# FiLM attention block and expert-choice block on one core: the order of the second layer's weight preparation and of the first norm

## The chip, the cores and the metric

The kernel runs on 1 core of one Trainium2 chip, as one launch. The metric is the device time in microseconds (us) of one execution; lower is better. Several executions of a kernel are given by their median.

A core has TensorE (PE, matrix products and transposes, into eight PSUM banks), VectorE (DVE), ScalarE (ACT), GpSimd (POOL) and SyncE (SP, which here only issues DMAs). The engines run side by side and are tied to each other by semaphores that the kernel sets and waits for by hand.

## The reference

x has the shape (2, 512, 128): two batches of 512 tokens of width 128. Two layers follow each other.

Layer 0: RMS norm, FiLM with a scale and a shift that come from `cond`, one attention head of width 128, its projection, the residual; then RMS norm, FiLM, and a GELU MLP 128 to 512 to 128 with its residual.

Layer 1, cut to what matters here:

```python
shift = silu(t) @ W_ada.T + b_ada
h = _ln(x, ln1_g, ln1_b) + shift
qkv = (h @ Wqkv.T).reshape(b, n, 3, H, HD)      # H = 16 heads, HD = 64
q, k = _ln(q, qn_g, qn_b), _ln(k, kn_g, kn_b)   # per head
attn = softmax(q @ k.T / sqrt(HD))              # per head
x = x + (attn @ v) @ Wout.T
```

Then a gate chooses 128 tokens for each of 8 experts (top-k by expert), the experts' two matrices with a GELU run on them, and the weighted results are added back to their tokens. All is float32.

## The kernel before

Every engine has one program, written in the order in which it runs. Tokens are kept in chunks of 128 (four to a batch). The stages are: load, layer 0 norm and FiLM, q, k and v of both batches, an attention loop over eight chunks (`g`), projection, the MLP (`up0`, `down0`), layer 1 norm, a hand-written lead-in to the heads, a loop over 32 units (16 heads by 2 batches), the gate, and the experts. Only what comes up to the lead-in, the first 84 us or so, is touched by the change.

**The start.** ScalarE issues the load of x as one DMA (L562) and squares it in two halves. VectorE sums the squares (`sum_squares`), GpSimd makes rstd (`norm_scale`, L451) behind its constants (L424 to L448), VectorE scales (`scaled`), and TensorE turns the four chunks of a batch (`turn_norm`). ScalarE (batch 0) or VectorE (batch 1) applies FiLM while copying out of PSUM (`into_h`). TensorE turns both batches ahead of the projections (L1292 to L1307), whose results are q0, k0 and v0. SyncE issues every other load in a fixed order (L377 to L394): early rows, film1, q, k, v, broadcast biases, Wqkv, W_ada, eleven pieces of the late rows, and the rest.

**The attention loop of layer 0.** In round g TensorE does `scores0(g)`, `turn0(g - 2)` and `mix0(g - 3)`; in round 1 it also turns the late rows (`late_turns`, L1270), which wait for their DMAs, and in round 3 it makes the products for FiLM 2 and `ada` (`late_products`). VectorE takes the row maximum and scales the probabilities, ScalarE makes the exponentials and copies turned probabilities.

**The weights of layer 1** are prepared in ten banks of 512 columns, n = 0 to 9. Banks 0 to 3 centre the q and k columns of Wqkv with a matrix product (`make_weights`, L1343): 0 and 2 hold heads 0 to 7, 1 and 3 hold heads 8 to 15. Banks 4 and 5 turn Wout (4: the part of heads 0 to 7). Banks 6 to 9 multiply each head's v weights by its part of Wout, with a contraction over 64 rows: 6 and 7 are even and odd heads of the first eight, 8 and 9 of the last eight. ScalarE copies each bank out (`copy_weights`, L594), into `w_hi` for q, k and v banks, and for these VectorE subtracts the copy to give `w_lo` (`weights_low`, L922). In TensorE's order banks 0 to 5 stand in rounds 1 to 6 of the loop, all through PSUM bank 7; bank 6 behind the loop, 7 behind `up0(3)`, 8 and 9 behind `down0(0)` and ahead of `up0(4)`. All ten are ready ahead of the first projection of layer 1.

**The lead-in.** `project(p, ...)` makes q, k and v for a head pair and two chunks, as three products (hi by hi, hi by lo, lo by hi). `piece_square`, `piece_ss`, `piece_scale`, `piece_norm`, `turn_piece`, `piece_affine`, `piece_high` and the low parts turn its result into normalized q and k. `project(0)` and `project(1)` take batch 0, `project(2)` and `project(3)` batch 1. Between the two pairs, batch 1's residual (`block_out(1)`), its centring (GpSimd, L532), its norm and `turn_norm(2, 1)` are done. `keep_busy(n)` does 4n transposes of the identity that nobody reads. `row_max` and `scores` are the first steps of the unit's attention. SyncE loads the experts' weights once the last half of h is split (`h_split` 4), which overwrites the raw weights.

Of the kernel before, what the change touches and what calls it, by code (L numbers as in the profile page):

```python
# [37 lines left out]
def film_attention_then_expert_choice(  # L38
# [35 lines left out]
    with ctx:  # L74
# [163 lines left out]
        proj_in = sem("proj_in")  # L238
# [16 lines left out]
        centring_ready, centre_ready = sem("centring_ready"), sem("centre_ready")  # L255
# [80 lines left out]
        def weight_bank(n):  # L336

            return bank[7] if n < QK_BANKS + WOUT_BANKS else bank[5 + n % 2]
# [10 lines left out]
        def weight_psum(n):  # L349

            return weight_bank(n)[:, :].rearrange("p (h d) -> p h d", d=HD if n < QK_BANKS else D)
# [24 lines left out]
        def _(sp):  # L376
# [27 lines left out]
            sp.wait_ge(wT_copied, W_BANKS + 1)  # L404
# [10 lines left out]
        def _(pool):  # L415
# [24 lines left out]
            pool.wait_ge(centring_ready, 1)  # L440
            link(pool.tensor_scalar(minus_ident[:, :], ident[:, :], -1.0, None, ALU.mult))
# [9 lines left out]
            def norm_scale(k, b, eps):  # L451
                pool.wait_ge(norm_ss, 2 * k + b + 1)
                at = slice(b * NC, b * NC + NC)
                link(pool.tensor_scalar(meansq[:, at], sumsq[:, at], 1.0 / D, eps, ALU.mult, ALU.add))
                pool.tensor_tensor(rstd[:, at], meansq[:, at], minus_half[:, at], ALU.pow).then_inc(norm_rstd, 1)  # L455

            norm_scale(0, 0, EPS0)
            norm_scale(0, 1, EPS0)

            pool.wait_ge(x_loaded, 16)  # L460
            pool.wait_ge(bcast_in, 48)
# [59 lines left out]
            def low_k(p):  # L521
# [39 lines left out]
        def _(act):  # L561
            act.dma_start(x_in[:, :, :], x.rearrange("b (c p) d -> p (b c) d", p=P)).then_inc(x_loaded, 16)  # L562
# [6 lines left out]
            square(x_in, 0)  # L569
            square(x_in, 1)  # L570
# [23 lines left out]
            def copy_weights(n):  # L594
                act.wait_ge(wT_done, n + 1)
                if n < QK_BANKS or n >= QK_BANKS + WOUT_BANKS:
                    act.activation(weight_part(w_hi, n), weight_psum(n), ACT.Copy).then_inc(wT_copied, 1)
                else:
                    m = n - QK_BANKS
                    act.activation(wout_T[:, 4 * m:4 * m + 4, :].rearrange("p c d -> p (c d)"),  # L600
                                   weight_bank(n)[:, :], ACT.Copy).then_inc(wT_copied, 1)
# [16 lines left out]
            copy_weights(QK_BANKS + WOUT_BANKS)  # L618
# [16 lines left out]
            for n in range(HC, 2 * HC):  # L635
                gelu0(n)
            act.wait_ge(wT_done, W_BANKS + 1)
            act.activation(wgate_T[:, :], bank[6][:, 0:E], ACT.Copy).then_inc(wT_copied, 1)
# [94 lines left out]
            for p in range(2):  # L733
                piece_square(p)
                piece_copy(p, p)
                piece_v(p, p)
# [9 lines left out]
            for half in range(2):  # L746
                at = half * (N // 2)
                act.activation(h_T[:, N + at:N + at + N // 2], bank[2][:, at:at + N // 2], ACT.Identity,
                               bias=affine[:, 2, 1, 1:2], scale=affine[:, 2, 0, 1:2]).then_inc(h_act, 1)
            q_high_beside(0, 0)  # L750
# [86 lines left out]
        def _(dve):  # L837
# [25 lines left out]
            sum_squares(0, 1)  # L863
            dve.wait_ge(cols_T, 1)
            dve.tensor_copy(cols[:, 0:EARLY], bank[0][:, 0:EARLY]).then_inc(cols_ready, 1)
            dve.wait_ge(cond_exp, 1)
# [3 lines left out]
            scaled(0, 0, x_in)  # L870

            def film_affine(k, film, fb, w):
                link(dve.tensor_scalar(affine[:, k, 0, :], film[:, 0:B], col(fb), 1.0, ALU.add, ALU.add))
                dve.tensor_scalar(affine[:, k, 0, :], affine[:, k, 0, :], col(w), None, ALU.mult)
                link(dve.tensor_scalar(affine[:, k, 1, :], film[:, B:2 * B], col(fb, 1), None, ALU.add))

            dve.wait_ge(film1_done, 1)
            film_affine(0, bank[4], "film1_b", "norm1_w")
            dve.tensor_copy(silu[:, 0, :], silu[:, 2, :]).then_inc(affine_ready, 1)
# [11 lines left out]
            def late_affine():  # L891
                dve.wait_ge(ada_done, 1)
                film_affine(1, bank[0], "film2_b", "norm2_w")
# [28 lines left out]
            def weights_low(n):  # L922

                dve.wait_ge(wT_copied, n + 1)
                dve.tensor_tensor(weight_part(w_lo, n), weight_psum(n), weight_part(w_hi, n).bitcast(F32),
                                  ALU.subtract).then_inc(w_split, 1)

            for g in range(TC + 1):
# [4 lines left out]
                if 2 <= g <= QK_BANKS + 1:  # L933
                    weights_low(g - 2)
# [18 lines left out]
            weights_low(QK_BANKS + WOUT_BANKS)  # L953
            sum_squares(1, 1)
            scaled(1, 1, x_mid)
            weights_low(QK_BANKS + WOUT_BANKS + 1)
            into_h(1)

# [9 lines left out]
            def split_h(lo, hi):  # L968
# [5 lines left out]
            at = slice(0, NC)  # L974
            block_out(0)
            link(dve.tensor_scalar(centre[:, at], centre[:, at], 1.0 / D, None, ALU.mult))
            dve.tensor_tensor(xn[:, at, :], x_att[:, at, :], spread(centre[:, at], [P, NC, D]), ALU.add)\
               .then_inc(norm_in, 1)
            weights_low(QK_BANKS + WOUT_BANKS + 2)
            sum_squares(2, 0)  # L980
            weights_low(QK_BANKS + WOUT_BANKS + 3)
            scaled(2, 0, xn)
            for half in range(2):
# [92 lines left out]
            scaled(2, 1, xn)  # L1076
            row_max(0, 0)
            dve.wait_ge(h_act, 5)
            split_h(N, N + N // 2)
            row_max(0, 1)  # L1080
            dve.wait_ge(h_act, 6)
            split_h(N + N // 2, TOK)
            row_max(0, 2)
# [157 lines left out]
        def _(pe):  # L1241
# [51 lines left out]
            turn_norm(0, 1)  # L1293
# [3 lines left out]
            for b in range(B):  # L1297
# [4 lines left out]
                pe.matmul(bank[5 + b][:, :], wk0[:, :], hb, start=True, stop=True).then_inc(qkv0_done, 1)  # L1302
                for c in range(NC):
# [39 lines left out]
            def make_weights(n):  # L1343
                dst = weight_bank(n)
                if n == 0:
# [3 lines left out]
                elif n <= QK_BANKS + WOUT_BANKS:  # L1349
                    pe.wait_ge(wT_copied, n)  # L1350
                    pe.wait_ge(w_split, min(n, QK_BANKS))
# [4 lines left out]
                elif n < QK_BANKS + WOUT_BANKS:  # L1356
                    if n == QK_BANKS:
# [428 lines left out]
```

## Time and profile before

| | us |
|---|---|
| median of 3 runs | 422.96 (422.95 to 424.42) |
| the profiled execution | 422.88 |
| its span, first to last instruction | 421.1 |
| TensorE busy | 399.4 (95%) |
| VectorE / ScalarE / GpSimd busy | 275.9 / 284.7 / 193.7 |

The profiled execution is one run of the program with the hardware profiler on. Its span is counted from the first to the last instruction of the core, and all times within the profile are from the span's start. In the profile PE is a matrix product or transpose, PEld a weight load, SPq and ACTq a DMA issued by that engine's queue. A float32 product appears as two instructions (two "passes"), so "x8" is a group of four products. A row of the timeline ends with the idle time ahead of it and what ended that, in brackets.

### The profile page before, as it was taken

What the parts mean: (1) busy time and instruction counts of PE and PEld (TensorE: products, weight loads), DVE (VectorE), ACT (ScalarE), POOL (GpSimd) and SP (SyncE); (2) the same over time, 40 slices, a digit from 0 to 9 for tenths busy, and PEclk for the clock granted to TensorE, in tenths of its full rate; (3) what the DMA queues carried; (4) which work ended last, traced back from release to release, by engine and by line L of the source; (5) the groups of instructions that cost most, each with busy time, mean ns of one, the idle gap of its engine ahead of it and who ended that gap; (6) DMA issues with size and microseconds to landing.
All of it is one profiled execution on the core that took longest, in us unless ns stands there. A gap on an engine that the chain in (4) does not pass through costs nothing.

```text
span 421.1 us, 8341 instructions
## 1 busy us (share of the span) xinstructions
PE 399.4 (95%) x2738; PEld 341.5 (81%) x2738; DVE 275.9 (66%) x648; ACT 284.7 (68%) x532; POOL 193.7 (46%) x203
## 2 busy tenths in 40 slices
PE   6999997899999999999999999999999997789996
PEld 5578666778899889989988998899898786566894
DVE  3666556776666676677676666766775736987733
ACT  3357566677788777778777887777777337759441
POOL 7500416485657756775776577567757000300000
PEclk9999999999999999999999999999999999999999
DMA  5760000191000000000000000000000000000001
GB/s 133 212 133 1 2 2 0 38 362 52 0 3 2 0 2 1 2 2 0 2 2 0 0 0 1 0 0 0 1 0 2 0 2 1 2 2 0 2 2 50
DMA packets 7792, 10.67 MB, mean 25 GB/s; under 512 B 403, under 2 KB 4302, under 8 KB 7758
## 3 DMA queue, kind: packets, MB, share of 16 engines
q1 hardware_dynamic: 6718, 9.73, 8.0%
q10 hardware_dynamic: 1040, 0.52, 0.4%
q8 instruction: 17, 0.28, 0.3%
q14 instruction: 17, 0.14, 0.1%
HBM read 8.68 MB, written 0.52 MB: 22 GB/s over the span
## 4 chain that ended last, share of the span: by engine, by line
PE 81%; DVE 10%; POOL 4%; issue 3%; ACT 2%; DVEq 0%; POOLq 0%; ACTq 0%
PE pair L1489 27%; PE pair L1440 10%; PE pair L1460 7%; PE bank L1479 6%; PE bank L1474 6%; PE pair L1245 4%; PE pair L1715 2%; PE pair L1727 2%; PE pair L1329 1%; PE pair L1405 1%; PE pair L1617 1%; PE bank L1245 1%; POOL rstd L455 1%; PE pair L1672 1%; PE pair L1354 1%
## 5 line engine op out<-in xcount | busy, mean ns | idle before, releaser
L1489 PE MATMUL pair<-v_s,probs_T 128*128 128x129 f32 x1024 | 128.4, 275 | 0.6 <-ACT probs_T L702 0.6
L1489 PEld LDWEIGHTS pair<-v_s,probs_T 128*128 128x128 f32 x1024 | 124.5, 191 | 4.6 <-ACT probs_T L702 0.9
L1016 DVE TENSOR_REDUCE negmax<-pair 128x1 f32<-128x512 f32 x128 | 88.5, 691 | 55.1 <-PE pair L1460 54.8
L702 ACT ACTIVATE probs_T<-bank 128x512 f32<-128x512 f32 x128 | 73.1, 597 | 48.7 <-PE bank L1479 39.4
L500 POOL TENSOR_TENSOR q_s<-kq,k_s 64x512 fp32r<-64x512 f32 x29 | 37.2, 1282 | 73.5 <-DVE k_s L1004 73.5
L1460 PE MATMUL pair<-k_s,q_s 128*128 128x512 f32 x128 | 56.4, 441 | 0.7 <-DVE negmax L1016 0.7
L490 POOL TENSOR_TENSOR qk_rstd<-qk_ms,minus_half 128x8 f32<-128x8 f32 x32 | 53.2, 1661 | 2.6 <-POOL qk_ms L486 0.2
L1474 PE MATMUL bank<-q_s,k_s 128*128 128x512 f32 x128 | 51.1, 399 | 0.0
L1479 PE MATMUL bank<-q_shift,k_low 128*128 128x512 f32 x128 | 50.7, 396 | 0.2 <-DVE q_shift L1023 0.2
L1038 DVE SCALAR_TENSOR_TENSOR x_att<-pair,o_rec,x_att 128x128 f32<-128x128 f32 x128 | 38.6, 344 | 1.1
L500 POOL TENSOR_TENSOR k_low<-kq,k_s 64x512 fp32r<-64x512 f32 x29 | 36.7, 1265 | 2.2
L1023 DVE TENSOR_TENSOR q_shift<-pair,own_chunk 4x512 fp32r<-4x512 f32 x32 | 21.8, 682 | 23.9 <-PE pair L1468 23.9
L509 POOL TENSOR_TENSOR qk_n<-qk_raw,qk_rstd 128x512 f32<-128x512 f32 x28 | 29.3, 1045 | 2.4 <-POOL qk_rstd L490 0.5
L1460 PEld LDWEIGHTS pair<-k_s,q_s 128*128 128x128 f32 x128 | 24.2, 189 | 6.0 <-DVE negmax L1016 3.1
L1479 PEld LDWEIGHTS bank<-q_shift,k_low 128*128 128x128 f32 x128 | 24.0, 188 | 5.7 <-issue 0.4
L650 ACT ACTIVATE qk_sq<-pair 128x512 f32<-128x512 f32 x32 | 19.2, 599 | 12.3 <-PE pair L1440 12.2
L1474 PEld LDWEIGHTS bank<-q_s,k_s 128*128 128x128 f32 x128 | 24.3, 190 | 3.0 <-ACT probs_T L702 0.5
L673 ACT ACTIVATE kq<-pair,cols 128x512 f32<-128x512 f32 x29 | 22.6, 778 | 4.5 <-PE pair L1245 1.4
L1440 PE MATMUL pair<-w_hi,h_hi 128*128 (+1 forms) x64 | 25.5, 398 | 0.0
L1440 PE MATMUL pair<-w_hi,h_lo 128*128 (+1 forms) x64 | 25.2, 394 | 0.0
L1440 PE MATMUL pair<-w_lo,h_hi 128*128 (+1 forms) x64 | 25.1, 391 | 0.0
L990 DVE TENSOR_REDUCE qk_ss<-qk_sq 128x8 f32<-128x512 f32 x32 | 21.7, 677 | 2.7 <-ACT qk_sq L650 2.7
(292 smaller groups left out, 697.5 us busy)
## 6 DMA issues: line engine op xcount, KB each, us to landing
fc_raw<-in_L_cond_fc2s_dram SPq DMA_DIRECT2D x1, 2048.0 KB, 13.8
x_in<-in_x_dram ACTq DMA_DIRECT2D x1, 512.0 KB, 3.9
w<-in_L_cond_mlp_w_dram SPq DMA_DIRECT2D x2, 256.0 KB, 2.9
wout<-in_L_cond_Wout_dram SPq DMA_DIRECT2D x1, 512.0 KB
k_low<-k_low SPq DMA_DIRECT2D x1, 512.0 KB, 8.0
q_shift<-q_shift SPq DMA_DIRECT2D x1, 512.0 KB, 9.4
b_all<-in_L_cond_b2s_dram SPq DMA_DIRECT2D x1, 512.0 KB, 10.9
out_dram<-final SPq DMA_DIRECT2D x2, 256.0 KB, 2.2
```

Source lines behind the costliest of these rows:

```text
L490: pool.tensor_tensor(qk_rstd[:, p_in % 2, :, :].rearrange("p c t -> p (c t)"), qk_ms[:, :, :].rearrange("p c t -> p (c t)"), minus_half[:, ...
L500: pool.tensor_tensor(piece_at(dst, p_in, lo, hi), kq32[lo:hi, :, :], piece_at(k_s, p_in, lo, hi).bitcast(F32), ALU.subtract)\
L509: pool.tensor_tensor(qk_n[:, p_in % 2, :, :, :], qk_raw[:, p_in % 2, :, :].rearrange("p c (t d) -> p c t d", d=HD), spread(qk_rstd[:, p_in ...
L673: act.activation(kq_from(p).rearrange("p h n -> p (h n)"), turn_bank(p)[:, :], ACT.Identity, bias=col("kq_b"), scale=col("kq_g")).then_inc ...
L702: act.activation(probs_T[:, k % 2, :], bank[2 + k % 2][:, :], ACT.Exp).then_inc(exp_done, 1)
L1016: dve.tensor_reduce(negmax[:, c:c + 1], bank[0][:, :], AX, ALU.max, negate=True).then_inc(max_done, 1)
L1038: last = dve.scalar_tensor_tensor(out=at, in0=pair4[:, half, t * (D + 1):t * (D + 1) + D], scalar=o_rec[:, c:c + 1], in1=at, op0=ALU.mult, ...
L1440: last = pe.matmul(banks_of(p)[:, c, :], h_part[:, at:at + P], w_part[:, bass.ds(head, 2), :].rearrange("p h w -> p (h w)"), start=(n == 0 ...
L1460: pe.matmul(bank[0][:, :], q_s[:, pair_at, h, c * P:c * P + P], k_s[:, pair_at, h, :], start=True, stop=True).then_inc(s_done, 1)
L1474: pe.matmul(bank[2 + k % 2][:, :], k_s[:, pair_at, h, at], q_s[:, pair_at, h, :], start=True, stop=False)
L1479: pe.matmul(bank[2 + k % 2][:, :], k_low[:, pair_at, h, at], q_shift[:, pair_at, h, :], start=False, stop=True).then_inc(st_done, 1)
L1489: last = pe.matmul(pair4[:, c // 2, c % 2 * (D + 1):(c % 2 + 1) * (D + 1)], probs_T[:, k % 2, c * P:c * P + P], v_s[:, r % (2 * PAIRS), k, :],
```

## The change

The ten banks are made in another order, `MADE`, and `make_weights`, `copy_weights` and `weights_low` count by the place in this order. Places 0 to 2 (banks 0, 2, 4) stand in rounds 1, 3 and 5 of the attention loop. Places 3 and 4 (V banks 6 and 7) are made together behind `up0(3)` by `make_v_weights(0)`, which goes through head pairs and alternates between the even head (rows 0 to 63) and the odd head (rows 64 to 127), each into a bank of its own. Place 5 (bank 1) stands behind `up0(7)`. Places 6 and 7 (banks 3 and 5) stand behind `project(1)`, and `make_v_weights(1)` (banks 8 and 9) between `turn_piece(0, 0)` and `turn_piece(1, 1)`. `project(3)` waits for all splits. The turn of Wgate gets semaphores of its own.

x comes in two DMAs, one for each batch. GpSimd takes the first two `norm_scale` ahead of five of its constants. VectorE copies the early columns ahead of batch 1's sum of squares and does FiLM ahead of silu. TensorE turns batch 1 between batch 0's k and v projections.

Of `down0(1)` one chunk is done ahead of `turn_norm(2, 0)` and three behind it, all ahead of `project(0)`; before, two stood ahead of `project(0)` and two behind `project(1)`. Batch 1's centring goes from GpSimd to VectorE and, with its sum of squares, ahead of piece 1's. ScalarE squares batch 1 ahead of the second piece. Groups of `keep_busy` are 3, 3, 4 and 1 where they were 3, 9 and 1, 2.

```diff
+        MADE = (0, 2, 4, 6, 7, 1, 3, 5, 8, 9)
+        def weight_bank(i):
+            return bank[(7, 7, 7, 5, 6, 7, 5, 2, 4, 5)[i]]
...
+            norm_scale(0, 0, EPS0)
+            norm_scale(0, 1, EPS0)
             link(pool.tensor_scalar(minus_ident[:, :], ident[:, :], -1.0, None, ALU.mult))
...
             piece_scale(1, 1, 0)
-            at = slice(NC, TC)
-            pool.wait_ge(centre_ready, 1)
-            pool.tensor_tensor(xn[:, at, :], x_att[:, at, :], spread(centre[:, at], [P, NC, D]), ALU.add)\
-                .then_inc(norm_in, 1)
+            norm_scale(2, 1, EPS1)
             low_k(0)
-            norm_scale(2, 1, EPS1)
...
-            act.dma_start(x_in[:, :, :], x.rearrange("b (c p) d -> p (b c) d", p=P)).then_inc(x_loaded, 16)
+            act.dma_start(x_in[:, 0:NC, :], x[0].rearrange("(c p) d -> p c d", p=P)).then_inc(x_loaded, 16)
+            act.dma_start(x_in[:, NC:TC, :], x[1].rearrange("(c p) d -> p c d", p=P)).then_inc(x_second, 16)
...
-                if 1 <= g <= QK_BANKS + WOUT_BANKS:
-                    copy_weights(g - 1)
+                if g in (1, 3, 5):
+                    copy_weights(g // 2)
...
             for n in range(HC):
                 gelu0(n)
-            for n in range(QK_BANKS + WOUT_BANKS + 1, W_BANKS):
-                copy_weights(n)
+            copy_weights(3)
+            copy_weights(4)
+            gelu0(HC)
+            gelu0(HC + 1)
             act.wait_ge(norm_in, 1)
             square(xn, 0)
...
-            piece_affine(0)
+            piece_square(0)
+            piece_copy(0, 0)
             act.wait_ge(norm_in, 2)
             square(xn, 1)
+            piece_square(1)
+            piece_copy(1, 1)
+            copy_weights(6)
+            piece_v(0, 0)
+            piece_affine(0)
+            copy_weights(7)
             q_high(0, 0)
+            piece_v(1, 1)
             piece_affine(1)
...
+            centred(1)
             piece_ss(0)
+            sum_squares(2, 1)
             piece_ss(1)
             piece_norm(0, 0)
-            block_out(1)
-            dve.tensor_scalar(centre[:, NC:TC], centre[:, NC:TC], 1.0 / D, None, ALU.mult).then_inc(centre_ready, 1)
+            weights_low(6)
+            piece_high(0, 0)
             piece_norm(1, 1)
-            piece_high(0, 0)
             low_here(0, HD, q_s).then_inc(q_low_done, 1)
-            sum_squares(2, 1)
+            scaled(2, 1, xn)
...
+            weights_low(8)
+            weights_low(9)
             row_max(0, 2)
...
+            def make_v_weights(eight):
+                first = (3, 8)[eight]
...
+                for k in range(4):
+                    pair_of = 4 * eight + k
+                    for odd in range(2):
+                        part = slice(odd * HD, odd * HD + HD)
+                        last = pe.matmul(weight_bank(first + odd)[:, k * D:k * D + D],
+                                         wqkv_raw[part, 2 * KC + pair_of, :], wout_T[part, pair_of, :],
+                                         start=True, stop=True)
...
-            make_weights(QK_BANKS + WOUT_BANKS + 1)
+            make_v_weights(0)
             turn_norm(1, 1)
             down0(0, range(NC))
-            for n in range(QK_BANKS + WOUT_BANKS + 2, W_BANKS):
-                make_weights(n)
...
+            make_weights(5)
...
+            down0(1, range(1))
             turn_norm(2, 0)
-            down0(1, range(NC // 2))
+            down0(1, range(1, NC))
...
             project(1, 1, 0)
-            down0(1, range(NC // 2, NC))
+            make_weights(6)
+            make_weights(7)
+            pe.wait_ge(norm_in, 2)
+            keep_busy(3, bank[4])
             turn_piece(0, 0)
-            keep_busy(3)
+            make_v_weights(1)
             turn_piece(1, 1)
-            keep_busy(9)
+            pe.wait_ge(v_placed, 2)
+            keep_busy(3, bank[1])
+            turn_norm(2, 1)
+            keep_busy(4, bank[1])
             scores(0, 0, 0)
-            turn_norm(2, 1)
...
-            pe.wait_ge(h_split, 4)
+            pe.wait_ge(w_split, SPLITS)
             project(3, 3, 0)
```

## Rows read from the trace of the kernel before

**Rows 1.** Busy time of the engines, and the granted clock in 40 slices, in tenths.
```profile
PE 399.4 (95%) x2738; PEld 341.5 (81%) x2738; DVE 275.9 (66%) x648; ACT 284.7 (68%) x532; POOL 193.7 (46%) x203
PEclk9999999999999999999999999999999999999999
```

**Rows 2.** Chain of waits, 0 to 90 us: start, duration (us), engine, tile, line.
```profile
17.35 0.86 PE bank L1314 x2
18.21 0.19 PE pair L1275
...
18.65 0.89 PE pair L1354 x8
...
40.62 1.85 PE pair L1329 x16
42.46 1.08 PE pair L1370 x8
...
50.84 3.59 PE pair L1405 x32
...
60.99 1.90 PE pair L1405 x16
62.89 1.40 PE pair L1440 x6
...
81.66 1.39 PE pair L1440 x6
83.05 0.24 PE pair L1460
```

**Rows 3.** Timeline of the start: start, duration, engine, line, operation, tiles.
```profile
4.74 1.15 ACT L566 ACTIVATE sq<-x_in 128x512 f32<-128x512 f32 x2 [2.18 <-DMA x_in<-in_x_dram]
...
6.33 0.23 POOL L448 TENSOR_SCALAR slot_number<-slot_number 128x1 f32<-128x1 f32 x1
...
6.72 5.83 SPq L386 DMA_DIRECT2D wada<-in_L_cond_W_ada_dram  x1
...
18.13 0.14 PEld L1275 LDWEIGHTS pair<-ident,late_rows 46*128 46x128 f32 x1 [0.76 <-DMA late_rows<-in_L_cond_qn_b_dram]
```

**Rows 4.** Timeline of the attention loop and behind it, 20 to 44 us.
```profile
21.05 0.68 DVE L925 TENSOR_TENSOR w_lo<-pair,w_hi 128x512 fp32r<-128x512 f32 x1
...
21.84 0.49 DVE L939 TENSOR_SCALAR p<-p,soft 128x512 f32<-128x512 f32 x1
...
21.88 1.13 PE L1354 MATMUL pair<-centring,wqkv_raw 128*128 128x128 f32 x8 [1.03 <-DVE w_lo L925]
...
42.66 0.69 DVE L854 TENSOR_TENSOR xn<-x_mid,rstd 128x512 f32<-128x512 f32 x1 [1.50 <-POOL rstd L455]
```

**Rows 5.** Timeline of TensorE: the last two V banks, and `slot_weights`.
```profile
54.34 1.71 PE L1370 MATMUL pair<-wout_T,wqkv_raw 64*128 64x128 f32 x16
...
388.31 0.63 PE L1686 MATMUL pair<-onehot,gate_parts 128*32 128x512 bf16 x8
```

**Rows 6.** Line 1686 alone: duration of one in ns, least, median and most.
```profile
L1686 PE MATMUL pair<-onehot,gate_parts x16: 386/392/400, 388.3 to 391.3; 128*32 128x512 bf16 x16
```

**Rows 7.** Timeline of the lead-in, 66 to 78 us, VectorE and GpSimd.
```profile
66.06 1.64 POOL L490 TENSOR_TENSOR qk_rstd<-qk_ms,minus_half 128x8 f32<-128x8 f32 x1
...
70.17 1.04 POOL L532 TENSOR_TENSOR xn<-x_att,centre 128x512 f32<-128x512 f32 x1
70.24 1.52 DVE L996 TENSOR_TENSOR qk_n<-qk_raw,qk_rstd 128x512 f32<-128x512 f32 x1 [0.29 <-POOL qk_rstd L490]
...
75.88 1.76 DVE L854 TENSOR_TENSOR xn<-xn,rstd 128x512 f32<-128x512 f32 x1 [0.91 <-POOL rstd L455]
```

**Rows 8.** Timeline of TensorE: transposes of the identity by `keep_busy`, early and late.
```profile
1.60 3.68 PE L1245 MATMUL pair<-ident 128*128 128x128 f32 x16 [1.60 <-POOL minus_half L427]
...
72.30 4.09 PE L1245 MATMUL pair<-ident 128*128 128x128 f32 x36
```

**Rows 9.** One stretch: busy us of PE, PEld, DVE, ACT, POOL; granted clock; DMA.
```profile
68.00:72.00 4.00, 2.16 (x18) 1.93 (x19) 3.64 (x6) 1.41 (x2) 3.13 (x3) 1.00 0.00 0
```

More of the change, by code:

```diff
@@ L334, in film_attention_then_expert_choice, with splits_ahead @@
         SPLITS = QK_BANKS + V_BANKS
-        def weight_bank(n):
-            return bank[7] if n < QK_BANKS + WOUT_BANKS else bank[5 + n % 2]
+        MADE = (0, 2, 4, 6, 7, 1, 3, 5, 8, 9)
+        assert len(MADE) == W_BANKS
+        def weight_bank(i):
+            return bank[(7, 7, 7, 5, 6, 7, 5, 2, 4, 5)[i]]
+        def splits_ahead(i):
+            return sum(n < QK_BANKS or n >= QK_BANKS + WOUT_BANKS for n in MADE[:i])
         def weight_part(t, n):
@@ L630, in _ @@
                 gelu0(n)
-            for n in range(QK_BANKS + WOUT_BANKS + 1, W_BANKS):
-                copy_weights(n)
+            copy_weights(3)
+            copy_weights(4)
+            gelu0(HC)
+            gelu0(HC + 1)
             act.wait_ge(norm_in, 1)
             square(xn, 0)
[L635 to L638, printed above, removed]
+            gelu0(HC + 2)
+            gelu0(HC + 3)
+            copy_weights(5)
+            act.wait_ge(wgate_done, 1)
+            act.activation(wgate_T[:, :], bank[6][:, 0:E], ACT.Copy).then_inc(wgate_copied, 1)
             act.wait_ge(norm_T, 5)
@@ L862, in _, with film_affine @@
             sum_squares(0, 0)
[L863 removed]
             dve.wait_ge(cols_T, 1)
             dve.tensor_copy(cols[:, 0:EARLY], bank[0][:, 0:EARLY]).then_inc(cols_ready, 1)
+            sum_squares(0, 1)
+            scaled(0, 0, x_in)
+            def film_affine(k, film, fb, w):
+                link(dve.tensor_scalar(affine[:, k, 0, :], film[:, 0:B], col(fb), 1.0, ALU.add, ALU.add))
+                dve.tensor_scalar(affine[:, k, 0, :], affine[:, k, 0, :], col(w), None, ALU.mult)
+                return dve.tensor_scalar(affine[:, k, 1, :], film[:, B:2 * B], col(fb, 1), None, ALU.add)
+            dve.wait_ge(film1_done, 1)
+            film_affine(0, bank[4], "film1_b", "norm1_w").then_inc(affine_ready, 1)
+            dve.wait_ge(affine_ready, 1)
             dve.wait_ge(cond_exp, 1)
@@ L869, in _ @@
             dve.tensor_tensor(silu[:, 2, :], silu[:, 1, :], cols[:, 0:B], ALU.mult).then_inc(silu_ready, 1)
[L870 to L879, printed above, removed]
+            dve.wait_ge(silu_ready, 1)
             scaled(0, 1, x_in)
@@ L972, in split_h, with centred @@
                    .then_inc(h_split, 1)
[L974 to L979, printed above, removed]
+            def centred(b):
+                block_out(b)
+                at = slice(b * NC, b * NC + NC)
+                link(dve.tensor_scalar(centre[:, at], centre[:, at], 1.0 / D, None, ALU.mult))
+                dve.tensor_tensor(xn[:, at, :], x_att[:, at, :], spread(centre[:, at], [P, NC, D]), ALU.add)\
+                   .then_inc(norm_in, 1)
+            centred(0)
             sum_squares(2, 0)
-            weights_low(QK_BANKS + WOUT_BANKS + 3)
             scaled(2, 0, xn)
+            weights_low(5)
             for half in range(2):
@@ L1360, in make_weights @@
                     last = turn4(dst, [wout[:, (at + c) * P:(at + c + 1) * P] for c in range(4)])
-                else:
-                    m = n - QK_BANKS - WOUT_BANKS
-                    if m < 2:
-                        pe.wait_ge(o0_copied, m + 1)
-                    else:
-                        pe.wait_ge(w_split, QK_BANKS + m - 1)
-                    for k in range(4):
-                        h = m // 2 * 8 + 2 * k + m % 2
-                        part = slice(h % 2 * HD, h % 2 * HD + HD)
-                        last = pe.matmul(dst[:, k * D:k * D + D], wqkv_raw[part, 2 * KC + h // 2, :],
-                                         wout_T[part, h // 2, :], start=True, stop=True)
-                last.then_inc(wT_done, 1)
+                last.then_inc(wT_done, 1)
+            def make_v_weights(eight):
+                first = (3, 8)[eight]
+                if eight == 0:
+                    pe.wait_ge(wT_copied, 3)
+                    pe.wait_ge(o0_copied, 2)
+                else:
+                    pe.wait_ge(wT_copied, 8)
+                    pe.wait_ge(w_split, splits_ahead(7))
+                for k in range(4):
[5 more added lines that the diff above has]
+                                         start=True, stop=True)
+                        if k == 3:
+                            last.then_inc(wT_done, 1)
             for g in range(TC + 3):
```

106 lines of the change are left out of this document (54 added, 52 removed).

## The prediction

> **What bounds the kernel now.** I read the page first: TensorE is busy nearly the whole span, at full granted clock [rows 1]. So the question is not which engine is busiest but what TensorE stands behind in the stretch that the change rewrites, from the start to about 84 us. From there on both kernels run the same loop, and what is won by then is carried to the end unchanged. The second view is the chain of waits over that stretch [rows 2]: nearly all of it is TensorE, with short handoffs to the other engines. Its pieces give the landmarks that I compare: the late rows' transposes at 18.21, the last mixes of the first attention ending at 42.46, `down0(0)` ending at 54.43, `project(0)` starting at 62.89, the score of chunk 3 of unit 0 at 83.05, right behind `project(3)`. The third view is the timeline, for who waits inside those pieces [rows 3 to 8].
>
> **Part 1, the start (x in two, Pool's constants later, batch 0 ahead): worth 0.** By itself it works. GpSimd can't take up the first norm before its constants end at 6.56, and ScalarE waits for the whole x [rows 3]. With half of x about 1 us earlier and the norm ahead of the constants, batch 0's projection starts near 8.9; with batch 1's turn behind q and k, all projections end near 14.8 instead of 16.5 (two scores of 0.86 ahead of 18.21 [rows 2]). But after these two scores TensorE comes to the late rows' transposes, which today are released at 18.13 by a DMA, the last of eleven small loads [rows 3]. SyncE issues those behind the load of `wada`, whose issue is held up for 5.83 us behind Wqkv [rows 3]. No issue of SyncE is moved and x carries the same bytes, so the release stays, and the 1.7 us become idle time in front of it. The cover is 1.7 us thick: if no part of the start worked, nothing would be lost. GpSimd's moved constants (from 3.7 to 6.56 today) end near 11, where it starts on x plus bias anyway.
>
> **Part 2, the loop of the first attention: -3.05.** Three of six banks leave it: two of eight passes (0.89 each [rows 2]) and one of four transposes (4 x 0.11 [rows 8]), 2.22 us of TensorE. With them goes the wait of the second bank for the low part of the first, 1.03 us [rows 4]: today both use bank 7 in successive rounds, afterwards a round lies between. VectorE loses two lows of 0.68 [rows 4] and ScalarE three copies, so neither becomes late instead. What is late next is `turn0(1)`: it needs the probability row whose scaling ends at 22.33 behind the first low [rows 4], as today, and restarts TensorE, 0.2 us. Sum 2.22 + 1.03 - 0.2 = 3.05. Played through round by round, `scores0` of round 3 starts at 20.8, of 4 at 25.4, of 5 at 27.6, of 6 at 30.2 (the late affine holds VectorE from 28.2 to 29.4, which makes round 6 wait for a probability row as well), of 7 at 32.5, and the last mix ends at 39.3, 3.1 ahead. The V bank at 42.46 (1.08) leaves too, but it covers a wait: the normalized x_mid arrives at 43.35 [rows 4]. Worth 0.05.
>
> **Part 3, the first V weights, sixteen passes instead of eight behind `up0(3)`: 0.15 gained or 0.7 lost.** Eight passes take 1.08 in the chain [rows 2]; sixteen, one half of the rows after the other, take 1.71 today [rows 5] and 1.8 with the restart. After the change each product alternates between rows 0 to 63 and rows 64 to 127, into different banks. If they overlap, sixteen passes take about 0.9. The nearest row for an overlap is `slot_weights`: eight 512-column matmuls in four column groups take 0.63 together [rows 5] though one alone lasts 0.39 [rows 6], while full-array ones of that length follow each other by 0.23 (six in 1.39 [rows 2]), 1.8 for eight. Column groups do overlap here; row groups never alternate in this trace. Bounds 0.9 and 1.8; I take 0.95, by that row. The Trainium skill says in TensorE: Matmul & The Clock Gate, Part 3, that a weight load passes a running matmul only where the row group differs, and gives a measured 3.07x for four row groups; in TensorEngine Tiling (Array Packing), Tiling Modes, it says that changing the tiling mode drains TensorE. The first would make the block 0.9; the second speaks against short blocks, and today's eight passes, 1.08 against 0.89 for eight full ones, would bear out 0.2 at most.
>
> **Part 4, from `down0(0)` to `project(0)`: 1.15 lost.** The two V banks in front of `up0(4)` go (1.71), but `up0` isn't the path there: the path is VectorE's block_out, centre and xn (three of 0.69 and a small one, 2.35), then square, sum, GpSimd, xn and turn, which stay. Into it falls ScalarE's new order, two gelus ahead of the square: two `up0` of 0.86, a handoff of 0.2 and the second gelu of 0.69 end 2.6 behind `down0(0)`, 0.25 later than xn. Behind the turn TensorE then does 24 passes of `down0(1)` instead of 16: another 8 x 0.112 = 0.9 (32 in 3.59 [rows 2]). The bank made there (0.89) and the Wgate turn lie in the wait for the square. If that wait weren't there they would cost 1.1.
>
> **Part 5, from `project(0)` to the score behind `project(3)`: 0.4 gained.** Today this is 20.16 us. After the change, counted from the start of `project(0)`: VectorE's centring of batch 1 ends at 2.25, the piece's sum of squares at 3.0, GpSimd's scale (0.3 + 1.64 [rows 7]) 5.0, norm 5.7, turn 6.4, affine 7.2, then ScalarE's copy of the second wout bank 7.8, for which the second V weights wait. These end at 9.7 (with 1.8) or 8.9 (with 0.9), `turn_piece(1)` 10.2, affine 11.0, high 11.7, low 12.4, the copy of k 13.0, half of h 13.6, its split 14.35, `project(2)` 15.9, the row maximum of chunk 1 16.8, two weight lows (2 x 0.68) on VectorE 18.2, and `project(3)` with handoffs 19.75. What goes is GpSimd's xn of 1.04 beside a norm that takes 1.52 instead of the 0.69 of this size, and part of 48 filler transposes; and batch 1's own norm, whose xn ends at 77.64 today [rows 7], comes some 4.5 us earlier and is no longer the path. What comes are the moved banks (0.89 + 0.44), the V weights and the lows. Batch 1's xn stretches to 1.76 today beside GpSimd's k_low [rows 7], and I leave it so; with that the overlap in the second V block is hidden but for 0.1.
>
> **Sum.** With overlap 3.05 + 0.05 + 0.15 - 1.15 + 0.4 = 2.5; without, 3.05 + 0.05 - 0.7 - 1.15 + 0.4 = 1.65. The profiled execution took 422.88 (span 421.1 and 1.8 around it), the median is 422.96. So **420.4** with overlap and 421.3 without. The experts' loads start some 3.5 us earlier, since they wait for the last split of h, and land long before they are read.
>
> **Rivals.**
> (a) *The row halves don't overlap.* For it: a pass with 64 rows costs today the 0.107 of one with 128 (1.71 / 16 [rows 5]). Against it: the column groups. 421.3. Chance 0.29.
> (b) *More is won: k_low doesn't meet xn.* Then xn is 1.07 shorter (0.69 [rows 4] for 1.76), of which 0.7 reaches the second piece's high part: 419.7. Against it: k_low stands right behind the rstd that xn waits for. Chance 0.14.
> (c) *Slower: TensorE's clock falls in the new gaps.* Sixteen transposes at the start take 3.68 (0.23 each), 36 at 72.3 take 4.09 (0.11 each) [rows 8]: the first run at 1.2 GHz, the others at 2.4. New are 1.7 idle us ahead of 18.13 and, near 69, a wait for the wout copy with fewer fillers. If each gap throws the clock down for as long as those sixteen and a little more, 4.3 us, each costs half of it, 2.15: 420.4 + 4.3 = 424.7. It decides from the first gap on; one gap alone gives 422.6, no change. Against it: between 68 and 72 TensorE is busy for 2.16 of 4 us today, at granted clock 1.00 [rows 9]. Chance 0.06, and 0.04 for one gap.
> (d) *The chain from 65 to 80 gives back more.* The weights aren't less work, only moved, and two lows in front of `project(3)` and a fuller ScalarE cost another 1.5 to 2: 422.2. For it: that stretch is a chain of single handoffs on VectorE and ScalarE, and one of them in the wrong order costs 0.7. Chance 0.09.
>
> **How the numbers follow.** My forecast has 0.38, (a) 0.29, (b) 0.14, (c) 0.10, (d) 0.09. About 0.5%, 2.1 us, is what a measurement of this kernel can tell from no change, so faster means under 420.8. The forecast lies 0.4 below that, (a) 0.5 above: faster takes four fifths of 0.38, a quarter of (a) and all of (b), 0.52; slower takes the two gaps of (c) and a little of (d), 0.07; the rest is 0.41. Range 419.2 to 422.4: down past (b) by a few terms of 0.1 to 0.2 that I rounded, up over (a) and (d).
>
> **What would show it.** Late rows at 18.1 with TensorE idle in front; last mix near 39.3; `down0(0)` ending near 51.2 (52.1 without overlap); `project(0)` near 60.8; the score of chunk 3 near 80.6, with `project(3)` waiting for the last low; sixteen V passes in 0.9 or 1.8. I am wrong if the late rows come at another time, if `project(0)` starts later than 61.7, if any transposes behind 18 us take 0.2, or if the time from that score to the end is not today's.

## The result and the profile after

The changed kernel takes **419.93 us** (median of 5, 419.68 to 420.69) against 422.96 before; the ratio is 0.9917 with a 95% interval from 0.9894 to 0.9941. The forecast was 420.4. Of the five runs of the kernel before three lie at 422.92 to 422.96 and two at 424.42 and 424.56; by the lowest times the gain is 3.24. The profiled execution took 419.68 with a span of 417.9, 3.2 less than before.

The page's first lines answer to [rows 1].

```profile
PE 396.0 (95%) x2722; PEld 338.1 (81%) x2722; DVE 275.2 (66%) x648; ACT 284.4 (68%) x532; POOL 192.8 (46%) x202
PEclk9999999999999999999999999999999999999998
```

TensorE has 3.4 us less of busy time, but this is not where the gain is read: a busy row includes filler transposes and pipelined overlap. It is read from landmarks. The chain of waits of the changed kernel (start, duration, what), beside [rows 2]:

```profile
6.71 6.11 SPq L394
...
16.52 1.21 DMA late_rows<-in_L_cond_qn_b_dram
17.73 0.04 issue
17.77 0.26 PE pair L1298
...
45.58 1.09 PE pair L1403 x16
...
47.26 3.57 PE pair L1439 x32
...
57.41 2.69 PE pair L1439 x24
...
76.98 1.21 DVE w_lo L943 x2
78.19 0.04 issue
78.23 1.66 PE pair L1475 x6
79.89 0.24 PE pair L1495
```

The chain now begins with SyncE's queue: up to 17.77 nothing but DMA issues and the landing of the last late row. And `project(3)` (L1475 at 78.23) stands behind two weight lows of VectorE (L943). Three more rows, from the timeline of TensorE and VectorE:

```profile
36.85 2.01 PE L1353 MATMUL pair<-pT,v 128*128 128x128 f32 x16
...
59.85 0.48 PE L1475 MATMUL pair<-w_hi,h_hi 128*128 128x512 f32 x1
...
69.44 1.76 DVE L870 TENSOR_TENSOR xn<-xn,rstd 128x512 f32<-128x512 f32 x1 [0.18 <-POOL rstd L454]
```

The landmarks as TensorE's rows have them in both traces. They lie up to 0.24 ahead of the chain's, which the prediction names, since passes of one group overlap those of the next; the intervals can be compared:

| | before | after | interval shorter by | forecast |
|---|---|---|---|---|
| late rows' transposes start | 18.14 | 17.77 | 0.37 | 0 |
| last mix of the first attention ends | 42.46 | 38.86 | 3.23 | 3.05 |
| `down0(0)` ends | 54.41 | 50.83 | -0.02 | 0.2 |
| `project(0)` starts | 62.65 | 59.85 | -0.78 | -1.15 |
| score of chunk 3 of unit 0 starts | 82.89 | 79.73 | 0.36 | 0.4 |
| span ends | 421.1 | 417.9 | 0.04 | 0 |

The sum is 3.2 against a forecast of 2.5. The forecast of the third row holds the 0.05 of the V bank at 42.46 beside the 0.15 of Part 3.

### The profile page after: what moved, and what is told of

Same layout as the page of the kernel before. It is cut to its first block, busy times and chain, and to the rows that moved or that the text cites. A ratio compares the mean times of both kernels' runs of the same rounds, so it can differ in the third digit from the quotient of the medians.

```text
span 417.9 us, 8313 instructions
## 1 busy us (share of the span) xinstructions
PE 396.0 (95%) x2722; PEld 338.1 (81%) x2722; DVE 275.2 (66%) x648; ACT 284.4 (68%) x532; POOL 192.8 (46%) x202
## 4 chain that ended last, share of the span: by engine, by line
PE 78%; DVE 10%; SPq 3%; issue 3%; ACT 2%; POOL 2%; DMA 0%; DVEq 0%; POOLq 0%; ACTq 0%
PE pair L1524 27%; PE pair L1475 10%; PE pair L1495 7%; PE bank L1514 6%; PE bank L1509 6%; PE pair L1268 4%; PE pair L1754 2%; PE pair L1766 2%; PE pair L1439 1%; SPq L394 1%; PE pair L1656 1%; PE pair L1353 1%; PE pair L1711 1%; DVE at_least L1159 1%; PE bank L1711 1%
## 5 line engine op out<-in xcount | busy, mean ns | idle before, releaser
L1475 PE MATMUL pair<-w_hi,h_hi 128*128 (+1 forms) x64 | 25.6, 400 | 1.1 <-DVE w_lo L943 0.6
L1475 PE MATMUL pair<-w_hi,h_lo 128*128 (+1 forms) x64 | 25.2, 394 | 0.0
L1475 PE MATMUL pair<-w_lo,h_hi 128*128 (+1 forms) x64 | 25.0, 391 | 0.0
```

What stands on the lines that cost most here:

```text
L1475: last = pe.matmul(banks_of(p)[:, c, :], h_part[:, at:at + P], w_part[:, bass.ds(head, 2), :].rearrange("p h w -> p (h w)"), start=(n == 0 ...
```

## Experiments

Times are medians, with lowest and highest in brackets. Because the runs of several kernels fall into groups up to 1.5 us apart (explained below by the clock), the lowest times are compared too. The changed kernel itself was not run again beside the experiments; the kernel before was, and its lowest times there, 422.74 to 422.79, are within 0.2 of the 422.92 above.

**The old start on the changed kernel.**

The edit, shortened:

```diff
-            act.dma_start(x_in[:, 0:NC, :], ...); act.dma_start(x_in[:, NC:TC, :], ...)
+            act.dma_start(x_in[:, :, :], ...)
-            norm_scale(0, 0, EPS0); norm_scale(0, 1, EPS0)      # ahead of minus_ident
+            ... behind slot_number, as before
-                if b == 0: turn_norm(0, 1)
+            turn_norm(0, 1)                                     # ahead of the projections
```

VectorE's part of the new start (the columns ahead of batch 1's sum of squares, FiLM ahead of silu) stays in, so this is the old start for ScalarE, GpSimd and TensorE alone.

> The changed kernel with the start of before: x in one DMA, GpSimd's constants ahead of the first norm, both batches turned ahead of the projections. Theory (the start is worth nothing, the late rows' DMA releases TensorE): the late rows' transposes start at 17.8 to 18.1 as in the changed kernel, TensorE hardly waits for them, and the time is 419.9 to 420.3. Rival (the start carries gain of its own, 1.7 us): late rows' transposes not the release, time near 421.6.

Measured 420.71 (419.81 to 421.6): 419.81, 419.91, 419.96 and 421.45, 421.5, 421.6. The lower three are 0.1 to 0.3 above the changed kernel's best, within what the theory gave. The upper three were expected by nothing. The profiled execution is one of them: its late rows' transposes start at 19.82, so where they start in the lower three, which the expectation names, is not shown. Its windows show what happened (columns: stretch, length, busy us of PE, PEld, DVE, ACT and POOL, granted clock, DMA share, GB/s):

```profile
8.00:10.00 2.00, 0.84 (x6) 0.42 (x4) 1.73 (x8) 0.59 (x1) 1.70 (x2) 1.00 0.24 64
10.00:12.00 2.00, 1.34 (x5) 1.25 (x6) 0.79 (x2) 0.19 (x1) 0.04 (x1) 0.65 0.90 288
12.00:14.00 2.00, 2.00 (x3) 0.67 (x2) 1.03 (x2) 0.00 (x0) 2.00 (x1) 0.50 1.05 295
```

Behind the waits for batch 0's and batch 1's norms the clock fell to 1.2 GHz until 14 us, and the projections ran at half rate. It need not fall there: in the profiled run of the kernel before, TensorE is busy for only 0.66 us from 8 to 10 and 1.39 from 10 to 12, and the granted clock is 1.00.

**Only the new start on the kernel before.** All that the change does to the start, VectorE's order included, and nothing else.

> The kernel before with only the new start: x in two DMAs, norm ahead of the constants, batch 0 projected ahead of batch 1's turn, nothing of the weights moved. Theory (covered by the late rows' DMA): TensorE idle some 1.7 us ahead of the late rows' transposes, 422.6 to 423.0; if x in two is what brought the late rows 0.4 earlier, 422.6 and transposes at 17.8. Rival (the start carries gain): 421.3.

Measured 423.44 (422.37 to 426.59, 12 runs), ratio 0.9996 (0.9974 to 1.0018). TensorE's rows up to the late transposes:

```profile
16.58 1.02 PE L1319 MATMUL bank<-kT,qT 128*128 128x512 f32 x2
17.87 0.26 PE L1279 MATMUL pair<-ident,late_rows 46*128 46x46 f32 x1 [0.28 <-DMA late_rows<-in_L_cond_qn_b_dram]
```

The transposes start 0.27 earlier than before and `project(0)` 0.25 earlier (62.40), and the lowest run is 0.37 below the lowest of before. The gap in front of them is only 0.3 here, because the scores start at 15.72, not 14.8. That isn't the edit: batch 0's xn starts at 6.53, as in the changed kernel (6.51), but the eight filler transposes ahead of it in TensorE's order take 1.97 from 5.40 on, where they take 1.47 in the changed kernel and 1.09 in the run with k_low behind xn, whose scores start at 14.80. In the changed kernel without its later fillers they take 1.97 too, and its scores start at 15.76. How early TensorE is done with the start thus differs by 1 us between executions. This execution, at 423.64, is also slower than any of this gain explains; where it lost the time is told below.

**Late rows' transposes one round later.** The same edit on the changed kernel and on the kernel before:

```diff
-                if g == 1:
+                if g == 2:
                     late_turns()
```

> The changed kernel with the late rows' transposes one round later in TensorE's order (round 2 instead of 1), so that the first weight bank and the scores of round 2 don't stand behind that DMA. Theory (the start's 1.7 us are real but stand idle in front of the late rows): about 1.0 us comes out, 418.7 to 419.2. Rival (something else, Wqkv's DMA or a probability row, is as late): 419.9, no change.

> The kernel before with the same single move of the late rows' transposes to round 2. Theory: before, TensorE came to them at 18.07 and was released at 18.13, so nothing is to be had: 422.8 to 423.2. Rival (the order of rounds 1 and 2 is worth something by itself): 422.0.

On the changed kernel: 419.35 (418.82 to 419.81), 0.9 below by lowest times. The last mix ends at 37.55, 1.3 earlier; so the start's time does stand idle in front of the late rows. The score of chunk 3 starts at 78.84, only 0.9 earlier, because the clock took the rest back between 64 and 72:

```profile
64.00:68.00 4.00, 2.27 (x22) 1.74 (x20) 2.88 (x5) 2.37 (x4) 3.83 (x4) 0.89 0.00 0
68.00:72.00 4.00, 4.00 (x27) 3.92 (x26) 2.87 (x3) 2.62 (x4) 2.72 (x3) 0.69 0.00 0
```

On the kernel before: 423.29 (422.46 to 426.03, 12 runs), 0.3 below by lowest times, with `project(0)` at 62.38, 0.27 earlier. The order of rounds 1 and 2 is thus worth a little even without the new start, and about 1.0 of the 1.3 is the start's. The medians, 0.6 below the changed kernel's and 0.4 above that of the kernel before beside it (422.91), mix groups of runs.

**V weights without alternation.**

```diff
-                for k in range(4):
-                    for odd in range(2):
+                for odd in range(2):
+                    for k in range(4):
```

> The changed kernel with the V weights' products in another order: first all four of the even heads (rows 0 to 63), then all four of the odd heads, instead of alternating. Theory (row halves overlap only when they alternate): the sixteen passes take 1.7 instead of 1.16, the first block moves everything behind it by 0.6, the second is partly hidden: 420.5 to 420.8. Rival (the short block comes from something else, such as the bank or the position): sixteen passes still 1.16, 419.9.

Measured 421.35 (420.15 to 422.83); the profiled execution took 420.43, the lowest is 0.5 above the changed kernel's. The sixteen passes, first this kernel's and then the changed kernel's:

```profile
45.61 1.71 PE L1403 MATMUL pair<-wout_T,wqkv_raw 64*128 64x128 f32 x16
```

```profile
45.51 1.16 PE L1403 MATMUL pair<-wout_T,wqkv_raw 64*128 64x128 f32 x16
```

The same products, banks and position: 1.71 against 1.16. The score of chunk 3 starts 0.72 later (0.11 of it with the late rows). The theory holds; products in alternating halves of rows overlap, by 1.5 and not by 2. One thing the run doesn't separate: each half has its own bank, so the changed kernel alternates banks as well, and this one doesn't. Against the bank speaks that full-array groups in different banks follow each other at the usual rate (the four transposes of `turn0`, and then `mix0` in another bank, start 0.44 apart, 4 x 0.11); alternating banks within one half was not run.

**Passes back into the attention loop, and the other engines' work back.**

```diff
+                if g in (2, 4, 6):
+                    pe.wait_ge(k0_ready, 2)
+                    keep_busy(1 if g == 6 else 2, bank[6])
```

> The changed kernel with filler transposes in rounds 2, 4 and 6 of the attention loop, of the length of the three banks that left it (8, 8 and 4 transposes), into a PSUM bank nobody reads and with no tie to ScalarE or VectorE. Theory (2.22 of the loop's 3.1 were TensorE's passes, 1.03 a wait that does not come back): last mix 2.2 later, 421.9 to 422.2. Rival (the rounds are paced by the handoffs between VectorE and ScalarE, and the passes fit beside them): under 421.

Measured 421.76 (421.24 to 422.68). In this run the late rows landed 1.0 later, so the loop is counted from their transposes to the last mix:

```profile
18.77 0.26 PE L1298 MATMUL pair<-ident,late_rows 46*128 46x46 f32 x1 [2.02 <-DMA late_rows<-in_L_cond_qn_b_dram]
...
39.13 2.01 PE L1353 MATMUL pair<-pT,v 128*128 128x128 f32 x16
```

This is 22.37, against 21.09 in the changed kernel and 24.32 before. The interval hardly depends on when the late rows land: it is 21.09 too in the runs of this section with late rows at 17.88, 18.03 and 19.82. The 2.2 us of passes cost 1.28, and the rows show where the other 0.9 went. The first line is the changed kernel's, the two others are this run's:

```profile
22.02 0.66 PE L1268 MATMUL pair<-ident,p 128*128 128x128 f32 x4 [0.68 <-DVE p L957]
```

```profile
21.31 1.04 PE L1268 MATMUL pair<-ident 128*128 128x128 f32 x8
23.04 0.62 PE L1268 MATMUL pair<-ident,p 128*128 128x128 f32 x4
```

The first eight passes stand where TensorE waits for a probability row anyway: `turn0(1)` comes 4.27 behind the late rows' transposes here and 4.25 in the changed kernel. The other twelve cost 1.26, their whole length. The expectation that the last mix moves by 2.2 fell.

The edit for the other engines, shortened:

```diff
+                if g in (2, 4, 6):     # ScalarE
+                    act.activation(spare, kT0[:, 0:N], ACT.Copy)
+                if g in (3, 5):        # VectorE
+                    dve.tensor_tensor(spare, v0[:, 0:NC, :], v0[:, NC:TC, :], ALU.subtract)
```

> The changed kernel with three extra 512-column copies on ScalarE (rounds 2, 4, 6) and two extra 512-column subtractions on VectorE (rounds 3, 5) of the attention loop, into tiles nobody reads: the copies and lows that left the loop, without TensorE's passes. The run with only the passes gave 1.3 of the loop's 3.2 back. Theory now (the rounds are paced by handoffs through VectorE and ScalarE as much as by TensorE): last mix 1 to 1.9 later, near 421.2. Rival (the rest is the wait for bank 7 alone, which neither brings back): last mix within 0.5 of the changed kernel's, 420.0.

Measured 420.27 (419.98 to 422.57). From 17.65 to the last mix at 39.02 it is 21.37, 0.28 more than the changed kernel. The rival holds: copies and lows alone cost next to nothing. (Two of the nine runs are at 422.4 and 422.6, with a mean granted clock of 0.988.) Passes 1.28 and copies with lows 0.28 leave 1.67 of the 3.23, which neither brings back by itself. No run put both back together, so that this is the tie between them, TensorE waiting for the copy and the low of a bank, is argued and not shown; but the rows say where most of it lies. From the late rows' transposes to `turn0(1)` it is 5.56 in the kernel before (18.14 to 23.70) and 4.27 with the passes back. These 1.29 hold the wait of 1.03 for the low part in bank 7 [rows 4].

**k_low behind xn.**

```diff
             norm_scale(2, 1, EPS1)
+            pool.wait_ge(norm_done, 6)
             low_k(0)
```

> The changed kernel with GpSimd's first k_low held back until batch 1's xn is written (a wait for norm_done 6). Theory (the two collide and xn stretches from 0.69 to 1.76; xn is on the path at 69.4 to 71.2): xn takes 0.69, the second piece's high part comes 0.7 earlier, 419.2 to 419.4. Rival (the path then goes through the second piece's affine on ScalarE, which ends at 70.4, or k_low collides with the next operation instead): 419.7 to 420.0.

Measured 420.98 (420.0 to 421.9). VectorE and GpSimd in this kernel:

```profile
69.68 0.69 DVE L871 TENSOR_TENSOR xn<-xn,rstd 128x512 f32<-128x512 f32 x1 [0.18 <-POOL rstd L454]
...
70.51 1.27 POOL L534 TENSOR_TENSOR k_low<-kq,k_s 64x512 fp32r<-64x512 f32 x1 [0.86 <-DVE xn L871]
...
70.69 1.37 DVE L1026 CAST k_s<-kq_second 128x512 fp32r<-128x512 f32 x1 [0.32 <-ACT kq_second L684]
```

xn is back at 0.69, and the cast behind it takes 1.37 instead of 0.41. The rival holds: the collision moves on, and nothing is won; `project(2)` starts 6.79 behind the second V block instead of 6.50. The time is above what the rival gave, too. Of the profiled execution's 1.2 us over the changed kernel 0.5 are there at the score of chunk 3; the other 0.7 come from a fall of the clock near 350 us, told below.

**No fillers ahead of the first unit.** Four `keep_busy` lines left out.

> The changed kernel without its four groups of filler transposes ahead of the first unit (11 x 4 transposes left out, nobody reads them). Theory (TensorE's clock does not fall in gaps of this size): transposes stay at 0.11 each, the time is 419.7 to 420.0. Rival (the fillers hold the clock at 2.4 GHz): passes of some stretch behind 64 us take twice as long and the time is 421 to 424.

Measured 422.65 (422.0 to 423.55, 12 runs), 2.7 above the changed kernel and 2.3 by lowest times. `project(2)` and `project(3)` in the chain, and the windows:

```profile
74.21 2.92 PE pair L1475 x6
77.14 0.44 PE pair L1495
79.54 2.93 PE pair L1475 x6
```

```profile
64.00:68.00 4.00, 0.87 (x8) 0.52 (x6) 2.36 (x5) 2.60 (x6) 3.69 (x5) 1.00 0.00 0
68.00:72.00 4.00, 2.27 (x24) 1.70 (x24) 3.76 (x5) 2.95 (x5) 2.98 (x3) 1.00 0.00 0
72.00:76.00 4.00, 2.58 (x5) 1.78 (x6) 2.06 (x6) 3.69 (x8) 1.24 (x1) 0.55 0.00 0
76.00:80.00 4.00, 2.79 (x6) 1.41 (x5) 2.40 (x4) 1.58 (x3) 0.00 (x0) 0.50 0.70 234
80.00:84.00 4.00, 4.00 (x17) 3.06 (x17) 1.80 (x4) 1.49 (x3) 1.84 (x2) 0.67 1.05 360
```

The theory fell. After two stretches in which TensorE was busy for 0.87 and 2.27 of 4 us, the clock fell to 1.2 GHz for some 10 us, and six passes took 2.92 instead of 1.66. In the changed kernel the fillers make these stretches 2.30 and 3.65, and the clock stays. 44 transposes that nobody reads are worth 2.3 to 2.7 us.

**A filler in the old start's gap, on the kernel before.**

```diff
             turn_norm(0, 0)
+            keep_busy(2)
             turn_norm(0, 1)
```

> The kernel before with eight filler transposes in TensorE's gap between the turns of batch 0 and of batch 1 (9.4 to 10.6 us). The runs of before fall into two groups, 422.8 and 424.4; the changed kernel with the old start does too (419.9 and 421.5), and its slow one has granted clock 0.5 to 0.65 from 10 to 14 us. Theory (the upper group is the clock that falls in this gap): all runs near 422.8, none near 424.4. Rival (the upper group has another cause, later in the kernel): both groups stay.

Measured 423.18 (422.87 to 425.41, 12 runs). Beside it the kernel before had 11 of 22 runs between 424.19 and 424.61; this one has none there: of its 12, five lie at 422.87 to 422.96, two at 423.0 and 423.3, four at 423.6 to 423.8 and one at 425.41. So the upper group hangs on this gap, and that it is the clock's fall fits: its 11 runs have a mean granted clock of 0.994 to 0.996, the other 11 one of 0.997 to 1.00. No run of the upper group of the kernel before was profiled; the profiled case is the changed kernel's with the old start.

For smaller steps the profiles show another place, far behind the change. (The runs at 423.6 to 423.8 above weren't profiled, so whether it is theirs is open.) The granted clock falls between 345 and 356 us (in one also from 360 to 365), around the start of the gate, in six of the profiled experiments: only the new start, k_low behind xn, no fillers, the other engines' work back, and the two that follow. The run with only the new start (423.64), and the kernel before:

```profile
350.00:360.00 10.00, 8.60 (x71) 7.43 (x71) 7.27 (x48) 7.17 (x29) 2.10 (x4) 0.83 0.00 1
```

```profile
350.00:360.00 10.00, 7.90 (x76) 6.28 (x75) 8.04 (x52) 7.15 (x30) 2.13 (x3) 1.00 0.01 2
```

From the score of chunk 3 to the end it is 338.1 to 338.3 us in the eight profiles that keep the clock there, and 338.2 to 340.6 in these six, 339.25 in this one. No edit touches that code.

**Late transposes and a filler, and with k_low held back.**

Both have the late rows' transposes in round 2 and this filler; the second also makes GpSimd wait for the second piece's low part of q:

```diff
             turn_piece(0, 0)
+            keep_busy(3, bank[4])
             make_v_weights(1)
...
             norm_scale(2, 1, EPS1)
+            pool.wait_ge(q_low_done, 2)
             low_k(0)
```

> The changed kernel with the late rows' transposes in round 2 and twelve filler transposes ahead of the second V weights, where TensorE stood idle 1.4 us and where the clock fell in the run with the late transposes alone (V passes 1.61 instead of 1.16). Theory (the clock falls there because the window of low activity got its phase wrong, and the fill prevents it): granted clock 1.00 from 60 to 84, V passes 1.16, 418.3 to 418.6. Rival (the fill doesn't change the clock, or costs its own length): 418.8 or more.

> The run with the late rows' transposes in round 2 and the filler, and GpSimd's first two k_low held back until the second piece's low part of q is written (a wait for q_low_done 2), so that neither batch 1's xn nor the cast behind it meets them. Theory: xn takes 0.69 and the cast 0.41, high part of piece 1 some 0.6 earlier, 417.7 to 418.0. Rival (k_low then collides with the splits of h behind, or ScalarE's affine is next): 418.3 to 418.8.

With the filler: 419.44 (418.3 to 420.89), ratio to before 0.989 (0.9865 to 0.9914). The clock is 1.00 from 60 to 72, V passes take 1.16, the score of chunk 3 starts at 78.34, 1.4 ahead of the changed kernel, and the two lowest runs (418.30, 418.31) are 1.4 ahead too. But two of six runs are at 420.7 and 420.9, and the profiled one of them lost its clock far behind, at unchanged code:

```profile
350.00:360.00 10.00, 7.86 (x72) 6.80 (x70) 8.19 (x38) 7.69 (x28) 3.91 (x9) 0.81 0.01 2
```

With k_low held back as well: 419.15 (418.79 to 421.32), lowest 0.5 above the other; its profiled run, at 421.32, lost 2.0 us near 350 as well. xn takes 0.69 and the cast 0.43, and then the cast that splits h meets k_low and takes 1.31 instead of 0.29; `project(2)` starts 7.05 behind the second V block instead of 6.51. The rival holds again.

## Why the prediction was right, and where its steps were off

**Direction and size.** The reasons held: work of heads 8 to 15 left a loop where it stood in line with everything, and went where TensorE waited anyway. The forecast was 0.5 too high, the sum 2.5 instead of 3.2. Two terms make the 0.7, the start (0.37) and Part 4 (0.37); the other differences cancel. By the number alone 419.93 lies nearer to rival (b)'s 419.7 than to 420.4, and (b)'s mechanism did not occur, so the number by itself would have pointed to the wrong cause. Some luck is in it as well: the forecast is counted from 422.96, and the median of the kernel before was 422.91, 423.85 and 424.3 beside the experiments, by how many of its runs fell into the upper group.

**Part 1 (0) was mis-sized: 0.37.** The late rows came at another time than 18.1, which I had named as a sign of being wrong. I took the row at 18.13 [rows 3] for a release by the DMA. But TensorE itself came there at 18.04, one score (0.86) behind the start of its second score at 17.18, and where it surely waits for no DMA, in the profile of the changed kernel with the old start, the transposes also start 0.95 behind that score's start (18.87 to 19.82). The last late row is issued at 16.24 in the kernel before; it lands 1.21 behind that issue in the changed kernel, and 1.36 and 1.37 in two experiments, so at 17.45 to 17.61, an estimate. So the start's gain reached TensorE until it met the DMA at 17.73. What I said of the remainder is right: `[0.77 <-DMA late_rows...]` stands in front of L1298, and the later turn takes 1.3 us out. The 0.37 is a difference of two executions: SyncE is held for 5.8 to 7.1 us at `wada`, and in the seven profiles with the new start and the turn in round 1 the transposes start between 17.65 and 18.77. (The loads of late rows are thirteen, not eleven.) And the start seems to do one thing that no step of mine had: the group of runs 1.5 us higher, half of the runs of before, is missing in the changed kernel's five.

**Part 2 (-3.05) measured 3.23, with the wrong split.** Up to `turn0(1)` my terms give 0.89 + 1.03 - 0.2 = 1.72, and the rows give 1.31 (5.56 less 4.25): I put what comes late next at 0.2, and TensorE stands 0.68 for that probability row. Behind it 1.92 are won instead of 1.33. The passes alone are worth 1.28 and not 2.22; the waits on the other two engines, the booked 1.03 among them, are the larger part.

**Part 3 was right in kind.** The rule from the Trainium skill, TensorE: Matmul & The Clock Gate, Part 3, that different row groups run together, agrees with the trace: 1.71 becomes 1.16. I took 0.95, by a row of four column groups in bf16; two groups of rows in float32 gave 1.16, so twice the passes cost what eight cost before (1.09 against 1.09 in the chain) instead of 0.15 less. Rival (a) is excluded: the changed kernel's own row has 1.16, and the order without alternation brings 1.71 back.

**Part 4 (1.15 lost) lost 0.78.** Two errors are in the term for the turn of ScalarE and the extra chunk: the second gelu ended at 53.28, 0.07 behind xn at 53.21, and not 0.25, since the handoff that I put at 0.2 is 0.02 in the chain; and eight further passes took 0.79 (2.69 - 1.90 [rows 2]) where I put 0.9. They make 0.29 of the 0.37.

**Part 5 (0.4) measured 0.36**, with the steps in the order given: xn of batch 1 at 1.76 beside k_low, `project(3)` behind the last low. Rival (d) is excluded by this. Rival (b) did not occur, and the two runs that forced it won nothing by it: in both placements k_low met the next VectorE cast instead.

**Rival (c)** had its condition nearly met. I argued against it from one stretch with 2.16 of 4 us at clock 1.00 [rows 9]. The fillers hold the clock; without them it costs 2.3 to 2.7. The other gap that I named, ahead of the late rows, threw the clock down in no profile, not even with 2.02 us idle.

## What to carry to other kernels

Work that prepares a later stage is cheapest where the engine waits anyway, but what it costs in a loop is its length less the waits it fills, plus the waits it brings: here 2.2 us of passes alone cost 1.3, and with the copies and lows tied to them 3.2. A wait that ends with a DMA in the profile is only then the DMA's when the engine was idle in front of it; compare when the engine itself arrived. Before taking filler out or moving work across a gap, look at the granted clock of many runs, not of one. And compare the stretch that an edit touches, from landmark to landmark, before the whole time: a fall of the clock 270 us behind it was larger here than some of the effects.

## What the hardware showed unexpectedly

The clock's fall is a matter of chance that code shifts: one kernel, the changed one with the old start, has three runs at 419.8 to 420.0 and three at 421.5 to 421.6, and the one of these that was profiled ran its first projections at 1.2 GHz, with 0.84 of 2 us busy in front. At the gate, in code that no edit touched, the clock fell in six of twelve profiled experiments and in neither of the two kernels' profiles. Matrix products of 64 rows that alternate between halves of the array (and between two banks) ran 1.5 times as fast as those in one half (16 passes in 1.16 against 1.71). A VectorE cast of 0.29 or 0.41 takes 1.31 or 1.37 when it meets a GpSimd subtraction of 1.27, about as if it waited for nearly all of it.
